# Graph layer on one core: the edge pass's hand-overs between TensorE, ScalarE and VectorE one third of a group later, a fourth one-hot buffer, chunks mixed from the middle third only

## Chip, cores and metric

The kernel runs on one NeuronCore of a Trainium2 chip. The metric is device time in microseconds. Before the change three runs took 1643.68, 1644.55 and 1645.81 us (median 1644.55). In the profile PE is TensorE (PEld its weight loads), ACT ScalarE, DVE VectorE, POOL GpSimd and SP SyncE; PEq, ACTq, DVEq, POOLq and SPq are their sequencers. "remote" and "another core or an unknown queue" both stand for a wait whose ending signal the profile can't put down to one instruction.

## The reference

There are 6250 nodes with 256 features and 106,250 edges sorted by destination. One layer computes

```
xn  = layernorm(x)
m   = xn[src] @ W[:256] + edge_attr @ W[256:]             # per edge
h   = segment_sum(m * rsqrt(degree)[dst], dst) + bias      # graph part
mix = gelu((q (K^T V)/N + xn) @ w1 + b1) @ w2 + b2 + xn    # linear attention, K and V normed per head
x   = x + h + mix
x   = x + expert_ffn(layernorm(x))                         # 2 of 8 experts, one choice for all nodes
```

The sum over edges is linear, so the kernel sums the raw gathered and edge rows by destination first and multiplies by W afterwards.

## The kernel before

There are three stages: a prologue (norms, a table of normed rows in memory), the edge pass, and the expert network. The change is in the edge pass.

**Steps and groups.** A strip is 128 x 3 edges, 4 strips make a group `t`, and there are 70 groups. A group has three steps, `q = 3t + i` with `i` 0, 1, 2. For a step SP loads four edge tiles (one DMA of 512 KB, line 423) and POOL gathers four tiles of 128 rows of 1 KB (four indirect DMAs, line 596) into one slot `q % 6` of a ring of six. PE multiplies the slot with one-hot matrices (`strip_sums`, lines 907 to 921) and then signals `s_seg`. SP and POOL may fill a slot again when `s_seg` says that the step six earlier is done (`wait_past(..., s_seg, q - RS + 1)`).

**What follows a group.** The group's sums stand in one of two PSUM banks. ACT copies them to `fl` (`evict`), PE transposes `fl` (`transposes`, line 927), ACT copies that to `fl_t` (`evict_t`), PE multiplies by W into the bank `ps_y` (`project`, lines 941 and 933, signals `s_pj`), and DVE adds the columns of `ps_y` to `acc` at a place read from a register (`sums`, line 1270, signals `s_acc`). The one-hot tiles `s32` are written by DVE for the next group (`one_hot`, line 1242), in three buffers.

**Work laid into the same steps.** Up to step 106 a tile of 125 nodes goes through keys and values every second step: `turn_kv` on PE, `turned` on ACT, `turned_lo` on DVE, `keys` on PE (line 986), `centred` on DVE, `squares` on ACT (line 704), `variances`, `deviations`, `normed`, `accumulate` on PE (992, 994). A short stretch folds the weights. Then 25 chunks of 250 nodes are mixed: `turn_mix` (1007), `turned`, `turned_lo`, `mix_first` (1020), `gelus` (723), `mixed_lo` (1308), `mix_second` (1030), `mixed` (1313), `store_base`. 25 times a chunk whose edge sums are complete is finished (`node_columns` 1043 and 1049, `degree_rows` 1359, `node_rows`, `row_scales`, `turn_rows` 1059 and so on).

**What sets the order.** Each engine runs its own copy of one loop over `q` and takes its instructions strictly in the order written there. `kv_at(q, lag)` and `mix_at(q, lag)` say which tile or chunk is `lag` steps old at `q`, `fin_at(t, lag)` the same in groups. So a number in the loops says in which step an engine turns to a piece of work, and what is written behind it in that step waits with it. Before the change in a group's steps:

```
        PE                                          ACT                       DVE
i = 0   sums, transposes(t-1)                       evict(t-1)                one_hot(t+1)
i = 1   sums, wait for acc, project(t-1)            evict_t(t-1)
i = 2   sums                                                                  sums(t-1)
```

A tile's transposes and keys are one step apart on PE (lags 0 and 1), a chunk's first and second product two (1 and 3). `MIX` holds the steps at which chunks begin: 114, 117, 121, 124, 128, 132, 135, 141, 144, ..., 201, from the eighth one on always at `i` = 0.

Of the kernel before, what the change touches and what calls it, by code (L numbers as in the profile page):

```python
# [14 lines left out]
P = 128  # L15
# [40 lines left out]
FOLD = KV0 + 2 * NT + 4  # L56
# [8 lines left out]
for c in range(NC):  # L65
    MIX.append(max(TS * FIRST - 3 + TS * 6 * c // 5, TS * (FIN[c - XC] + 5) if c >= XC else 0))
# [11 lines left out]
def gps_layer(nc, x, src_l, dst_l, edges, wgnn, hbias, wkv_l, wq_t, bkv_l, bq_l, kln_g, kln_b, vln_g, vln_b,  # L78
              w1, b1_l, w2, b2, wr, br, fw1, fb1_l, fw2, fb2, gamma, beta, out):
    ctx = ExitStack()  # L80
    with ctx:
# [34 lines left out]
        s32 = sbe("s32", [P, 3, GT, W], F32R)  # L116
# [539 lines left out]
        def _(act):  # L656
# [116 lines left out]
            for q in range(TS * STEPS):  # L773
# [17 lines left out]
                if kv_at(q, 3) is not None:  # L791
                    deviations(kv_at(q, 3))
# [6 lines left out]
                if mix_at(q, 5) is not None:  # L799
                    store_base(mix_at(q, 5))  # L800
# [95 lines left out]
        def _(pe):  # L896
# [12 lines left out]
            def strip_sums(q):  # L909
# [8 lines left out]
                for j in strips(t):  # L918
                    mm = pe.matmul(ps_seg[t % 2][j * W:(j + 1) * W, :], lhsT=s32[:, t % 3, j * TS + i, :].bitcast(F32), rhs=ring[:, u, j, :],  # L919
                                   start=i == 0, stop=i == TS - 1, skip_group_check=True)  # L920
# [16 lines left out]
            def project(t):  # L937
                n = W * len(strips(t))
                hot = s32[:, t % 3, :, :].rearrange("p (j i) w -> p j i w", i=TS)
# [122 lines left out]
            for q in range(TS * STEPS):  # L1062
# [3 lines left out]
                if i == 0 and 1 <= t <= NG:  # L1066
                    transposes(t - 1)
                if i == 1 and t:
                    columns_free(t)
                    if fin_at(t, 0) is not None:  # L1070
                        pe.wait_ge(s_acc, min(strips_before(DONE[fin_at(t, 0)]), NS))
                        node_columns(fin_at(t, 0))
                if i == 1 and 1 <= t <= NG:
                    if t == 1:
                        pe.wait_ge(s_par, 16 * 11)
                    project(t - 1)
                if kv_at(q, 5) is not None:
                    accumulate(kv_at(q, 5))
                if kv_at(q, 0) is not None:
                    turn_kv(kv_at(q, 0))  # L1080
                if kv_at(q, 1) is not None:
                    keys(kv_at(q, 1))
                if q in (FOLD + 1, FOLD + 3, FOLD + 5):
                    fold_weights((q - FOLD) // 2)
                if mix_at(q, 3) is not None:
                    mix_second(mix_at(q, 3))
                if mix_at(q, 0) is not None:
                    turn_mix(mix_at(q, 0))
                if mix_at(q, 1) is not None:
                    mix_first(mix_at(q, 1))  # L1090
                if i == 2 and fin_at(t, 2) is not None:
                    turn_rows(fin_at(t, 2), mixes_turned(q))

# [91 lines left out]
        def _(v):  # L1185
# [51 lines left out]
            def one_hot(t):  # L1237
# [3 lines left out]
                wait_past(v, s_pj, t - 2)  # L1241
                v.tensor_tensor(s32[:, t % 3, 0:m, :], iota[:, 0:W].unsqueeze(1).broadcast_to([P, m, W]),
# [156 lines left out]
            for q in range(TS * STEPS):  # L1399
# [5 lines left out]
                if i == 0 and fin_at(t, 1) is not None:  # L1405
                    node_rows(fin_at(t, 1))
                if kv_at(q, 4) is not None:
                    normed(kv_at(q, 4))
                if kv_at(q, 2) is not None:
                    centred(kv_at(q, 2))  # L1410
                if kv_at(q, 3) is not None:
                    variances(kv_at(q, 3))
                if i == 2 and 1 <= t <= NG:
                    v.wait_ge(s_pj, t)
# [219 lines left out]
```

## Time and profile before

| | |
|---|---|
| Profiled execution, own time | 1625.46 us |
| Its span, first to last instruction | 1623.7 us |
| Median of the timed runs | 1644.55 us |
| Mean granted TensorE clock | 0.868 of full speed |
| Busy over the span | PE 1182.9, POOL 935.0, DVE 637.4, ACT 546.5 us |
| Gathers (POOL, line 596) | 831, 803.3 us busy, 967 ns each, first at 52.0, last at 1275.2 us |
| One-hot products (PE, line 919) | 1662, 294.5 us busy |
| Projection (PE, line 933) | 1120, 157.2 us busy |
| Expert network (lines 1145 and 1156) | from about 1336 us to the end |

A row of the timeline gives start and length in us, engine, line, operation, what it writes and reads, how many were merged, and in brackets how long the engine sat idle before it and what ended that. A row of the waits gives who waited for whom, the total in us, the number and the longest.

### The profile page before, as it was taken

What the parts mean: (1) busy time and instruction counts of PE and PEld (TensorE: products, weight loads), DVE (VectorE), ACT (ScalarE), POOL (GpSimd) and SP (SyncE); (2) the same over time, 40 slices, a digit from 0 to 9 for tenths busy, and PEclk for the clock granted to TensorE, in tenths of its full rate; (3) what the DMA queues carried; (4) which work ended last, traced back from release to release, by engine and by line L of the source; (5) the groups of instructions that cost most, each with busy time, mean ns of one, the idle gap of its engine ahead of it and who ended that gap; (6) DMA issues with size and microseconds to landing.
All of it is one profiled execution on the core that took longest, in us unless ns stands there. A gap on an engine that the chain in (4) does not pass through costs nothing.

```text
span 1623.7 us, 22761 instructions
## 1 busy us (share of the span) xinstructions
PE 1182.9 (73%) x7416; PEld 804.4 (50%) x7416; DVE 637.4 (39%) x1619; ACT 546.5 (34%) x1126; POOL 935.0 (58%) x1005
## 2 busy tenths in 40 slices
PE   0257777677768676766676767777777839999997
PEld 0024344334334343334444544453554539999997
DVE  6113232233233233312234333342342446676775
ACT  5401111111111111111233333432443457677674
POOL 6566666666666666666666666666666103334342
PEclk9968888888889887877788788899887959999999
DMA  9956666666666666476677777777877341222221
GB/s 271 291 173 185 181 198 200 181 188 194 192 193 192 195 188 187 146 234 212 203 224 236 247 230 234 245 225 252 243 234 236 104 136 39 74 59 76 66 66 39
DMA packets 209236, 295.04 MB, mean 182 GB/s; under 512 B 20940, under 2 KB 180146, under 8 KB 207887
## 3 DMA queue, kind: packets, MB, share of 16 engines
q1 hardware_dynamic: 152899, 165.66, 34.4%
q0 software_dynamic: 39888, 108.97, 22.1%
q10 hardware_dynamic: 16350, 19.20, 3.6%
q8 instruction: 48, 0.79, 0.2%
q14 instruction: 51, 0.42, 0.1%
HBM read 261.75 MB, written 32.00 MB: 181 GB/s over the span
## 4 chain that ended last, share of the span: by engine, by line
PE 31%; another core or an unknown queue 27%; issue 19%; ACT 8%; DVE 8%; DMA 2%; DVEq 2%; SPq 1%; POOL 1%; ACTq 0%; POOLq 0%
PE bank L1145 8%; PE bank L1156 8%; PE bank L919 3%; PE bank L933 2%; PE bank L1030 2%; DVEq L1268 2%; ACT fl L658 2%; PE bank L927 1%; DVE lnst L1287 1%; PE bank L986 1%; ACT L743 1%; ACT L723 1%; ACT fl_t L658 1%; PE bank L992 1%
## 5 line engine op out<-in xcount | busy, mean ns | idle before, releaser
L596 POOL DMA_INDIRECT ring<-xn_table,src_sb x831 | 803.3, 967 | 431.8 <-issue 232.0
L919 PE MATMUL bank<-ring,s 128*32 128x512 f32 x1662 | 294.5, 686 | 72.2 <-DMA ring<-xn_table,src_sb 49.1
L933 PE MATMUL bank<-fl_t,wg 128*128 128x128 f32 x1120 | 157.2, 298 | 38.3 <-issue 24.9
L933 PEld LDWEIGHTS bank<-fl_t,wg 128*128 128x128 f32 x1120 | 144.9, 209 | 42.2 <-issue 26.6
L1270 DVE TENSOR_TENSOR acc<-acc,bank 128x96 f32 x277 | 70.7, 255 | 224.5 <-issue 86.2
L927 PE MATMUL bank<-ident,fl 128*128 128x128 f32 x280 | 58.1, 343 | 136.8 <-ACT fl L658 114.6
L927 PEld LDWEIGHTS bank<-ident,fl 128*128 128x128 f32 x280 | 37.3, 170 | 215.8 <-ACT fl L658 151.2
L1275 DVE TENSOR_TENSOR xt_lo<-bank,xt_hi 128x250 fp32r<-128x250 f32 (+1 forms) x75 | 37.8, 505 | 270.0 <-ACT xt_hi L658 195.4
L658 ACT ACTIVATE xt_hi<-bank 128x250 fp32r<-128x250 f32 (+1 forms) x75 | 33.4, 445 | 297.9 <-remote 237.3
L919 PEld LDWEIGHTS bank<-ring,s 128*32 128x32 f32 x1662 | 43.0, 114 | 169.0 <-issue 163.0
L1145 PE MATMUL bank<-xf_hi,fw_hi 128*128 128x256 f32 x400 | 113.6, 284 | 9.5 <-DVE fw_lo L1572 7.2
L986 PE MATMUL bank<-wkv_hi,xt_hi 128*125 128x512 f32 x100 | 56.4, 564 | 87.1 <-DVE xt_lo L1275 87.1
L704 ACT ACTIVATE kvn<-xc 125x512 f32<-125x512 f32 x50 | 31.5, 630 | 259.8 <-DVE xc L1283 131.0
L647 POOL TENSOR_TENSOR rx<-vex,half 125x2 f32<-125x2 f32 x25 | 17.7, 707 | 171.9 <-DVE nmx L1546 171.9
L1525 DVE TENSOR_TENSOR h_lo<-h,h_hi 128x512 fp32r<-128x512 f32 x100 | 95.7, 968 | 48.7 <-ACT h_hi L658 48.7
L1145 PE MATMUL bank<-xf_lo,fw_hi 128*128 128x256 f32 x400 | 113.8, 284 | 0.0
L1145 PE MATMUL bank<-xf_hi,fw_lo 128*128 128x256 f32 x400 | 113.4, 283 | 0.0
L1156 PE MATMUL bank<-fw_hi,h_hi 128*125 128x256 f32 x400 | 111.7, 279 | 0.0
L1156 PE MATMUL bank<-fw_hi,h_lo 128*125 128x256 f32 x400 | 111.7, 279 | 0.0
L1156 PE MATMUL bank<-fw_lo,h_hi 128*125 128x256 f32 x400 | 111.6, 279 | 0.0
L844 ACT ACTIVATE h<-bank,fb1c 128x256 f32<-128x256 f32 x200 | 83.4, 468 | 73.2 <-PE bank L1145 72.7
L1283 DVE TENSOR_TENSOR xc<-bank,bkv 125x512 f32<-125x512 f32 x50 | 34.6, 692 | 147.4 <-remote 70.1
(213 smaller groups left out, 2349.7 us busy)
## 6 DMA issues: line engine op xcount, KB each, us to landing
ring<-edges SPq DMA_DIRECT2D x207, 512.0 KB
ring<-xn_table,src_sb POOLq DMA_INDIRECT x831
xnr<-xn_table SPq DMA_DIRECT2D x50, 125.0 KB
xnr<-xn_table SPq DMA_DIRECT2D x25, 250.0 KB
xch<-x SPq DMA_DIRECT2D x25, 250.0 KB
base_rows<-xch ACTq DMA_DIRECT2D x25, 250.0 KB
x_rows<-xch ACTq DMA_DIRECT2D x25, 250.0 KB
xt_cols<-xte ACTq DMA_DIRECT2D x25, 250.0 KB
```

Of the source, the lines that this page charges most:

```text
L596: pool.indirect_dma_start(out=to, out_offset=None, in_=table, in_offset=bass.IndirectOffsetOnAxis(ap=index, axis=0),).then_inc(done, 16)
L658: return nc.scalar.activation(o, i, ACT.Copy)
L844: nc.scalar.activation(h32[:, f, :], bank[q][:, (f % 2) * CW:(f % 2 + 1) * CW], ACT.Gelu, bias=fb1c[:, f:f + 1]).then_inc(s_gel, 1)
L919: mm = pe.matmul(ps_seg[t % 2][j * W:(j + 1) * W, :], lhsT=s32[:, t % 3, j * TS + i, :].bitcast(F32), rhs=ring[:, u, j, :], start=i == 0, ...
L927: mm = pe.transpose(ps_t[:, c * P:(c + 1) * P], fl[:, c * P:(c + 1) * P], ident[:, :])
L933: mm = pe.matmul(ps_y[:, o * P:(o + 1) * P], lhsT=wg[:, c, o * P:(o + 1) * P], rhs=fl_t[:, c, :], start=c == 0, stop=c == 3)
L986: mm = pe.matmul(ps_kv[0:TN, :], lhsT=a, rhs=b, start=i == 0, stop=i == len(ops) - 1)
L1145: mm = pe.matmul(bank[q][:, (f % 2) * CW:(f % 2 + 1) * CW], lhsT=a, rhs=b, start=n == 0, stop=n == len(ops) - 1)
L1156: mm = pe.matmul(ps_o[u][0:TN, j * D:(j + 1) * D], lhsT=a, rhs=b, start=n == 0, stop=n == len(ops) - 1)
L1270: v.tensor_tensor(acc[:, :, ds(b, W)], acc[:, :, ds(b, W)], ps_y[:, 0:3 * P].rearrange("p (c n) -> p c n", c=3)[:, :, j * W:(j + 1) * W], ...
L1275: v.tensor_tensor(xt_lo[:, :, 0:width], ps_xt[:, 0:KC * width].rearrange("p (c n) -> p c n", c=KC), xt_hi[:, :, 0:width].bitcast(F32), ALU ...
L1525: v.tensor_tensor(h_lo[:, u, 2 * q:2 * q + 2, :], h32[:, 2 * q:2 * q + 2, :], h_hi[:, u, 2 * q:2 * q + 2, :].bitcast(F32), ALU.subtract).t ...
```

## The change

Each hand-over inside the group and inside a tile or chunk is asked for later, the one-hot tiles get a fourth buffer (`HOT = 4`, the wait in `one_hot` becomes `s_pj >= t - 3`), and `MIX` becomes 115, 118, 121, 124, 127, 133, 136, 142, ..., 202: always at `i` = 1. `FOLD` is one step later. PE's wait for `acc` before the projection is split off: `columns_free` waits only for `s_acc`, the degree signal `s_dr` is waited for before `project` alone.

```
        PE                                          ACT                       DVE
i = 0   sums, ..., project(t-2) last in the step    evict(t-1)                one_hot(t+1)
i = 1   sums, transposes(t-1)                                                 ..., sums(t-2) last
i = 2   sums, node_columns                          evict_t(t-1)
```

A tile's lags on PE are now 0, 2 and 6 (before 0, 1 and 5), a chunk's 0, 2 and 5 (before 0, 1 and 3); ACT and DVE move with them. What each operation computes, the DMAs, their sizes and the ring of six are as before.

```diff
-FOLD = KV0 + 2 * NT + 4
+HOT = 4
+FOLD = KV0 + 2 * NT + 5
-    MIX.append(max(TS * FIRST - 3 + TS * 6 * c // 5, TS * (FIN[c - XC] + 5) if c >= XC else 0))
+    MIX.append(max(TS * (FIRST + c + c // 5) - 2, TS * (FIN[c - XC] + 5) + 1 if c >= XC else 0))
@@ ACT
-                if i == 1 and 1 <= t <= NG:
+                if i == 2 and 1 <= t <= NG:
                     evict_t(t - 1)
-                if i == 1 and fin_at(t, 1) is not None:
+                if i == 2 and fin_at(t, 1) is not None:
                     store_rows(fin_at(t, 1))
-                if kv_at(q, 2) is not None:
-                    squares(kv_at(q, 2))
+                if kv_at(q, 3) is not None:
+                    squares(kv_at(q, 3))
-                if mix_at(q, 2) is not None:
-                    gelus(mix_at(q, 2))
+                if mix_at(q, 3) is not None:
+                    gelus(mix_at(q, 3))
@@ PE
-                wait_past(pe, s_acc, strips_before(min(t, NG - 1) - 1) if t < NG else strips_before(NG - 1) + (1 if t > NG else 0))
-                wait_past(pe, s_dr, sum(g < t for g in FIN))
+                wait_past(pe, s_acc, min(strips_before(t), NS))
-                if i == 0 and 1 <= t <= NG:
+                if i == 1 and 1 <= t <= NG:
                     transposes(t - 1)
-                if i == 1 and t:
-                    columns_free(t)
-                    if fin_at(t, 0) is not None:
-                        pe.wait_ge(s_acc, min(strips_before(DONE[fin_at(t, 0)]), NS))
-                        node_columns(fin_at(t, 0))
-                if i == 1 and 1 <= t <= NG:
-                    project(t - 1)
-                if kv_at(q, 5) is not None:
-                    accumulate(kv_at(q, 5))
+                if i == 2 and fin_at(t, 0) is not None:
+                    columns_free(t - 1)
+                    pe.wait_ge(s_acc, min(strips_before(DONE[fin_at(t, 0)]), NS))
+                    node_columns(fin_at(t, 0))
+                if kv_at(q, 6) is not None:
+                    accumulate(kv_at(q, 6))
+                if kv_at(q, 2) is not None:
+                    keys(kv_at(q, 2))
                 if kv_at(q, 0) is not None:
                     turn_kv(kv_at(q, 0))
-                if kv_at(q, 1) is not None:
-                    keys(kv_at(q, 1))
-                if mix_at(q, 3) is not None:
-                    mix_second(mix_at(q, 3))
+                if mix_at(q, 5) is not None:
+                    mix_second(mix_at(q, 5))
+                if mix_at(q, 2) is not None:
+                    mix_first(mix_at(q, 2))
                 if mix_at(q, 0) is not None:
                     turn_mix(mix_at(q, 0))
-                if mix_at(q, 1) is not None:
-                    mix_first(mix_at(q, 1))
+                if i == 0 and 2 <= t <= NG + 1:
+                    columns_free(t - 2)
+                    wait_past(pe, s_dr, sum(g < t for g in FIN))
+                    project(t - 2)
@@ DVE
-                wait_past(v, s_pj, t - 2)
+                wait_past(v, s_pj, t - HOT + 1)
-                if i == 2 and 1 <= t <= NG:
-                    v.wait_ge(s_pj, t)
-                if i == 2 and fin_at(t, 0) is not None:
-                    degree_rows(fin_at(t, 0))
-                if i == 2 and 1 <= t <= NG:
-                    sums(t - 1)
+                if i == 1 and 2 <= t <= NG + 1:
+                    sums(t - 2)
```

On DVE `degree_rows` moves to `i` = 0 of the following group, `node_rows` to `i` = 1, `normed`, `centred` and `variances` one step later each, `mixed` and `mixed_lo` two.

## Rows read from the trace of the kernel before

**Rows 1.** Windows: stretch, us; busy PE, PEld, DVE, ACT, POOL; clock, DMA, GB/s.

```profile
325.00:500.00 175.00, 129.95 (x681) 68.57 (x682) 57.63 (x142) 27.93 (x66) 114.55 (x120) 0.84 0.64 192
...
745.00:920.00 175.00, 123.10 (x750) 79.40 (x750) 57.55 (x170) 53.02 (x102) 115.99 (x119) 0.80 0.73 223
...
920.00:1095.00 175.00, 129.60 (x798) 83.71 (x795) 64.90 (x194) 65.40 (x135) 114.92 (x118) 0.89 0.77 236
```

**Rows 2.** Waits of POOL, whole execution: us in total, times, longest.

```profile
POOL ring L596 <- issue: 232.0, 738, 1.0
...
POOL ring L596 <- remote: 142.7, 67, 5.2
...
POOL ring L596 <- PE bank L919: 46.1, 25, 4.7
```

**Rows 3.** Waits of all engines, 150 to 1265 us.

```profile
ACT xt_hi L658 <- remote: 223.7, 35, 13.5
...
ACT hm L723 <- remote: 136.0, 16, 14.2
...
PE bank L927 <- ACT fl L658: 112.8, 34, 9.3
...
PE bank L986 <- DVE xt_lo L1275: 86.5, 15, 7.7
```

**Rows 4.** Timeline, 422 to 431 us, keys-and-values stretch.

```profile
422.08 0.38 PE L975 MATMUL bank<-ident,xnr 125*128 125x125 f32 x2
...
422.39 1.06 PE L919 MATMUL bank<-ring,s 128*32 128x512 f32 x8
...
426.74 0.95 POOL L596 DMA_INDIRECT ring<-xn_table,src_sb  x1 [0.30 <-issue]
...
430.04 0.38 ACT L658 ACTIVATE xt_hi<-bank 128x250 fp32r<-128x250 f32 x1 [9.72 <-remote]
...
430.37 0.94 POOL L596 DMA_INDIRECT ring<-xn_table,src_sb  x1 [2.68 <-remote]
...
430.93 0.79 PE L986 MATMUL bank<-wkv_hi,xt_hi 128*125 128x512 f32 x1 [6.00 <-DVE xt_lo L1275]
```

**Rows 5.** The timeline, 447 to 450 us, the next group.

```profile
447.60 0.69 DVE L1283 TENSOR_TENSOR xc<-bank,bkv 125x512 f32<-125x512 f32 x1 [7.08 <-remote]
...
449.12 0.59 ACT L658 ACTIVATE fl<-bank 128x512 f32<-128x512 f32 x1
...
449.76 1.12 PE L927 MATMUL bank<-ident,fl 128*128 128x128 f32 x4 [3.90 <-ACT fl L658]
```

**Rows 6.** The timeline, 1012 to 1034 us, mixing stretch.

```profile
1012.13 0.60 ACT L658 ACTIVATE fl<-bank 128x512 f32<-128x512 f32 x1 [9.78 <-remote]
...
1012.88 0.66 PE L927 MATMUL bank<-ident,fl 128*128 128x128 f32 x4
...
1029.70 0.83 ACT L723 ACTIVATE hm<-bank,bm 128x250 f32<-128x250 f32 x2 [9.66 <-remote]
...
1032.61 0.58 ACT L658 ACTIVATE fl<-bank 128x512 f32<-128x512 f32 x1
...
1033.24 1.11 PE L927 MATMUL bank<-ident,fl 128*128 128x128 f32 x4 [1.77 <-ACT fl L658]
```

**Rows 7.** The timeline, 419 to 421 us: one projection on PE.

```profile
419.85 0.55 PE L941 MATMUL bank<-s,ones_r 128*128 128x128 f32 x3
...
420.24 2.00 PE L933 MATMUL bank<-fl_t,wg 128*128 128x128 f32 x16
```

**Rows 8.** The chain that ended last: start us, us, what.

```profile
813.35 2.12 PE bank L1020 x12
...
1050.24 2.56 PE bank L1030 x12
...
1335.97 7.42 PE bank L1145 x48
```

**Rows 9.** The timeline, the last gather.

```profile
1275.18 0.94 POOL L596 DMA_INDIRECT ring<-xn_table,src_sb  x1 [4.72 <-PE bank L919]
```

More of the change, by code:

```diff
@@ L115, in gps_layer @@
         ring = sbe("ring", [P, RS, ST, 2 * D])
-        s32 = sbe("s32", [P, 3, GT, W], F32R)
+        s32 = sbe("s32", [P, HOT, GT, W], F32R)
         ones_r = sbe("ones_r", [P, P], F32R)
@@ L786, in _ @@
                     norm_rows(fin_at(t, 2))
-                if kv_at(q, 2) is not None:
-                    squares(kv_at(q, 2))
+                if kv_at(q, 3) is not None:
+                    squares(kv_at(q, 3))
                 if kv_at(q, 0) is not None:
                     turned(kv_at(q, 0), TN)
-                if kv_at(q, 3) is not None:
-                    deviations(kv_at(q, 3))
+                if kv_at(q, 4) is not None:
+                    deviations(kv_at(q, 4))
                 if q == FOLD + 6:
                     mix_weights()
-                if mix_at(q, 2) is not None:
-                    gelus(mix_at(q, 2))
+                if mix_at(q, 3) is not None:
+                    gelus(mix_at(q, 3))
                 if mix_at(q, 0) is not None:
                     turned(NT + mix_at(q, 0), CN)
-                if mix_at(q, 5) is not None:
-                    store_base(mix_at(q, 5))
+                if mix_at(q, 7) is not None:
+                    store_base(mix_at(q, 7))
                 if i == 2 and fin_at(t, 1) is not None:
@@ L918, in strip_sums @@
                 for j in strips(t):
-                    mm = pe.matmul(ps_seg[t % 2][j * W:(j + 1) * W, :], lhsT=s32[:, t % 3, j * TS + i, :].bitcast(F32), rhs=ring[:, u, j, :],
+                    mm = pe.matmul(ps_seg[t % 2][j * W:(j + 1) * W, :], lhsT=s32[:, t % HOT, j * TS + i, :].bitcast(F32), rhs=ring[:, u, j, :],
                                    start=i == 0, stop=i == TS - 1, skip_group_check=True)
@@ L938, in project @@
                 n = W * len(strips(t))
-                hot = s32[:, t % 3, :, :].rearrange("p (j i) w -> p j i w", i=TS)
+                hot = s32[:, t % HOT, :, :].rearrange("p (j i) w -> p j i w", i=TS)
                 for i in range(TS):
@@ L1405, in _ @@
                 if i == 0 and fin_at(t, 1) is not None:
+                    degree_rows(fin_at(t, 1))
+                if i == 1 and fin_at(t, 1) is not None:
                     node_rows(fin_at(t, 1))
+                if kv_at(q, 5) is not None:
+                    normed(kv_at(q, 5))
+                if kv_at(q, 3) is not None:
+                    centred(kv_at(q, 3))
                 if kv_at(q, 4) is not None:
[L1408 to L1412, printed above, removed]
-                if i == 2 and 1 <= t <= NG:
-                    v.wait_ge(s_pj, t)
-                if i == 2 and fin_at(t, 0) is not None:
-                    degree_rows(fin_at(t, 0))
-                if i == 2 and 1 <= t <= NG:
-                    sums(t - 1)
+                    variances(kv_at(q, 4))
                 if kv_at(q, 0) is not None:
@@ L1422, in _ @@
                     fold((q - FOLD) // 2)
-                if mix_at(q, 4) is not None:
-                    mixed(mix_at(q, 4))
+                if mix_at(q, 6) is not None:
+                    mixed(mix_at(q, 6))
                 if mix_at(q, 1) is not None:
                     base_rows(mix_at(q, 1))
-                if mix_at(q, 2) is not None:
-                    mixed_lo(mix_at(q, 2))
+                if mix_at(q, 4) is not None:
+                    mixed_lo(mix_at(q, 4))
                 if mix_at(q, 0) is not None:
                     turned_lo(NT + mix_at(q, 0), CN)
+                if i == 1 and 2 <= t <= NG + 1:
+                    sums(t - 2)
             v.wait_ge(s_acc, NS)
```

6 lines of the change are left out of this document (3 added, 3 removed).

## The prediction

> **What bounds the kernel now.** I read the page first for the stages, then the windows, the waits of POOL, the waits of all engines, and last the timeline of single groups. The expert network begins at 1336 us with PE in one unbroken row [rows 8] and is not touched, so all that can move is the edge pass, from the first gather at 52.0 to the last at 1275.2 us [rows 9]. That is 831 gathers, 69.25 groups of 12, and so 17.66 us a group. The windows show no engine full: of 175 us (ten groups) PE is busy 123 to 130, POOL 115, ACT 28 to 65, DVE 58 to 65, the DMA engines 0.64 to 0.77 [rows 1]. PE's busy time is the same 12 to 13 us a group in both halves, and so is the group's time.
>
> POOL is nearest to a floor. A gather takes 967 ns on average (the page) and 0.30 us lie between two [rows 4], so 12 of them need 15.2 us. The rest is in its waits for a ring slot: 142.7 us ended by "remote" and 46.1 by the one-hot products, 92 waits in all [rows 2]. Both are the same wait, for `s_seg`. Less the 0.30 us that stands between gathers anyway, 188.8 - 92 x 0.30 = 161 us. That is the most the change can win as long as POOL issues 831 gathers.
>
> So POOL waits for PE. Does PE wait for data? No: it is six steps behind POOL, a full ring. The timeline shows what it does wait for. At 422.08 it turns a tile (0.38 us), at 422.39 it sums a step, but ACT takes the turned tile up only at 430.04, POOL its slot at 430.37, and PE's keys start at 430.93 [rows 4]. Such late answers are the largest waits of the pass: ACT on the turned tile 223.7 us in 35 waits, ACT on the chunk's first product 136.0 in 16, PE on `fl` 112.8 in 34, PE on `xt_lo` 86.5 in 15 [rows 3]. I take two parts in them apart: the time until PE's signals are out (here 430.0, when ACT and POOL go on within 0.4 us of each other), and the time after it in which PE stands until ACT and DVE have answered.
>
> **The change part by part.** No work is added to the loops but the width of one buffer. Every instruction, DMA and wait on a ring slot is there as often as before; the price of the moves is in waits alone.
>
> *Hand-overs.* PE asks now for `fl` after the next step's sums instead of in front of them, for `fl_t` two steps and not one after `fl`, and for `xt_lo` two steps after the turn. What goes is the stand after the signals are out. Its size, from single groups: 430.93 - 430.04 = 0.9 us (keys) [rows 4]; 449.76 - 447.60 = 2.2 us, the chain DVE `xc`, ACT square, ACT `fl` [rows 5]; in the mixing stretch 1012.88 - 1012.13 = 0.75 and 1033.24 - 1029.70 = 3.5 us, the latter with ACT's gelus, a table load and a root in front of `fl` [rows 6]. The mean is 1.5 us a group over the 31 groups from 150 to 700 us and 2.1 over the 30 from 745 to 1265: 47 + 63 = 110 us. The low end of this term is 0: if POOL's wait ends only with the burst of signals, PE's earlier idling costs nothing. The high end is the whole of POOL's waits, 161 us. I take half of the 110, 55 us, because the two groups in rows 4 and 5 both show POOL released in the burst itself (430.37, and DVE at 447.60), and not by a step of its own that PE did after waiting for ACT; only what PE has done before the next burst counts, and that is where a shorter stand helps.
>
> *Projection last in step 0, sums last in step 1, fourth one-hot buffer.* The projection takes 0.55 + 2.00 us with the small gap between, 2.4 us [rows 7], as before. DVE's four additions begin one step later than the projection instead of in the next but one place; `one_hot(t+1)` waits for projection t-2, which then stands 3 steps back, so it waits for nothing. Cost 0 beside the ring; without the fourth buffer DVE would wait at each group's start for the projection that PE does at the end of that very step. The bounds are a gain of 0.5 us a group, if DVE's order was late, and a loss of the same: 0 +- 30 us. I take 0.
>
> *Chunks.* `mix_second`, `mix_first` and the projection now all stand in step 0: sums 1.06, second 2.56, first 2.12, projection 2.4 [rows 4, 7, 8] make 8.1 us in which one slot comes free, against 5.0 us for POOL's four gathers of a step. Before, the longest such stretch was step 1 with sums, projection and first product, 5.6 us. The sum per group is the same, and the other two steps become shorter; it costs nothing as long as the ring has a slot in hand, and up to 2.5 us a chunk if it has none, 25 x 2.5 = 63 us. I take 0 for the likeliest case because the stretch after it is shorter by as much, and keep the 63 for a rival.
>
> *SP.* `mix_load` is asked for at step `MIX[c]`, its three waits (turns, `base_rows` of two chunks ago, stored rows of six chunks ago) keep their distance in steps; edge loads queue behind it as before. 0.
>
> *End.* Two steps later for the last group's projection and additions, on a nearly idle machine: between the last gather at 1275.2 and the network at 1336 lie 61 us. One projection and four additions stand in the way at most once more, some 5 us. On the other side PE is less far behind when the gathers end. I take +5.
>
> Sum: -55 + 0 + 0 + 5 = -50 us. The profiled execution took 1625.5 us by its own time, 19 us less than the median of the timed runs, 1644.55, and no difference in the stages is seen for it here; I subtract the 50 from the median: **1595 us** (profiled: 1575).
>
> Two rules of the Trainium skill bear on the split. The page "SBUF — State Buffer", section "SBUF: two separate sides", says that DMA and the engines reach SBUF by separate ports and cannot slow each other. By that rule the 7.6 us in rows 4 between PE's turn and ACT's copy are no matter of the gathers in flight, all waits are hand-over, and the second rival below is the likeliest; the trace does not plainly agree, since at 422.4 to 430.0 ACT and PE had nothing else to do. "Perfetto Trace Analysis", section "Optimization Strategy", says that the same gap repeating on an engine that should be full can mean too few buffers for the next tile. POOL's repeating wait agrees with it, the ring keeps its six slots, and by this rule nothing is won: the first rival.
>
> **The rivals.**
>
> *The waits come back elsewhere (the ring decides).* POOL waits 92 times in 69 groups, 2 us at a time on average, in the stretch of keys as in that of chunks, although the work on PE, ACT and DVE is quite different [rows 1, 2]. That speaks for a cycle of its own: ring full, POOL stops, PE's signals come in a burst, POOL goes on. Then a group stays at 17.6 us and the time at 1640 to 1650. Against it: in both bursts shown PE stood idle before it, so more could have been done by then.
>
> *POOL becomes the bound.* Every hand-over has a whole step of 5 us now, more than the answers measured. If that ends most of POOL's waits, a group takes 15.2 to 16 us, -161 to -100 with the end: 1488 to 1545, say 1525. For it: PE's 12 to 13 us of work fit into 15.2. Against it: the 7.6 us for PE's signals in rows 4 are longer than one step, and moving work doesn't shorten them.
>
> *Slower: step 0 too full.* The mechanism is the 8.1 us of PE work in step 0 of the mixing stretch. It decides when PE's slot signals are still a full ring behind at that point, which the waits say they are in nearly all groups before. Then POOL waits up to 2.5 us more in each chunk, up to 63 us, against at best a part of the 63 us that shorter hand-overs give there; and the 47 us of the first half come only in part if the signals are late. Taken at a third of the 63 with nothing won elsewhere, +21: 1665; at most 1705. The smaller idle time of PE against it would have to be seen in the first half.
>
> **How the numbers follow.** Chances: forecast 0.43 (its own range 1560 to 1620); POOL the bound 0.14; ring decides 0.20; step 0 too full 0.18; the moves do little things of either sign, within 20 us, 0.05. A measurement of this kernel tells 0.2% (3.3 us) from no change. Of the ring case 0.12 lie within that, 0.05 on the faster side and 0.03 on the slower; the last case is shared. Faster 0.43 + 0.14 + 0.05 + 0.03 = 0.65, same 0.12, slower 0.18 + 0.03 + 0.02 = 0.23. The range leaves out the lower half of POOL the bound and the worse half of step 0 too full: 1522 to 1664.
>
> **What would show it.** Right: POOL's waits on line 596 other than "issue" fall from 189 us to some 130; last gather near 1225 us; PE no longer waits for `fl` and `xt_lo` (199 us now) but the copies on ACT still start late after PE; a group 16.9 us. The ring case: the waits for `fl` and `xt_lo` go, POOL's stay at 189, PE's idle time moves to other lines or in front of line 919. POOL the bound: last gather before 1180 us. Step 0 too full: the windows before 700 us no longer than now, those after 745 us longer, POOL's waits there ended by line 919 and longer than the 4.7 us of now. I am wrong altogether if DVE or ACT show a new long wait, on `s_acc`, on `s_dr` or on a root, in front of the projection.

## The result and the profile after

The changed kernel takes 1667.69 us (median, 1663.83 to 1670.97) against 1644.12 for the kernel before beside it: a ratio of 1.0159, 95% interval 1.0138 to 1.018, slower by 24 us by the medians and 26 by the ratio. The forecast was 1595. All comparisons leave out one execution, of e18's kernel, that took 2598.55 us where its others took 1494 to 1504. The profiled execution after took 1667.02 us, near its median; the one before, 1625.46, was 19 us quicker than its own, so the two traces show 41.5 us of difference where some 25 are to be explained.

By stage, read from the starts of POOL's gathers (from a group's first gather to another group's first gather, and the last gather) and of DVE's mean over the nodes, which the expert network waits for. The labels e1 to e18 are the experiments told below; "quick set" is explained at e14.

| us | group 0 to 35 | 38 to 68 | last gather to mean | mean to end |
|---|---|---|---|---|
| before | 611.2 | 532.5 | 33.0 | 315.5 |
| before, a second profile (e7) | 609.4 | 530.8 | 33.2 | 315.0 |
| after | 618.2 | 547.2 | 51.2 | 314.8 |
| e1, group's part | 614.4 | 547.4 | 46.4 | 314.4 |
| e2, keys' part | 614.7 | 537.6 | 33.0 | 315.2 |
| e3, chunks' part | 617.5 | 535.2 | 43.2 | 315.1 |
| e4, additions first | 613.8 | 540.8 | 51.9 | 315.2 |
| e5, projection first too | 608.3 | 535.2 | 50.9 | 316.4 |
| e6, chunks earlier | 610.8 | 540.7 | 41.3 | 316.3 |
| e9, all three moves | 613.9 | 542.1 | 43.1 | 314.9 |
| e10, keys' part, chunks earlier | 614.1 | 547.6 | 33.0 | 315.6 |
| e12, before, ring of five | 615.4 | 541.7 | 32.5 | 315.3 |
| e14, before, half rows, quick set | 535.0 | 459.1 | 27.3 | 314.3 |
| e16, keys' part, quick set | 534.4 | 476.4 | 35.4 | 315.4 |
| e18, changed, quick set | 536.5 | 478.5 | 50.8 | 314.8 |

The tail after the last gather is the steadiest item: +18 us. The two long stretches are not steady. The kernel before, e12 and e10 time alike (within 0.1% of each other), and yet their first stretch differs by up to 6 us and their second by up to 17 (530.8 to 547.6). The 547.2 us of the changed kernel lie inside that, so one profile's stretch does not show a loss of this size. What does is the timed ratio less the tail: 26 - 18 leaves some 8 us, with the ratio's interval 4 to 11, for everything in front of the last gather.

The windows of the kernel after, the same stretches as in [rows 1] (stretch; busy time of PE, weight loads, DVE, ACT, POOL; clock, DMA share, GB/s):

```profile
325.00:500.00 175.00, 134.31 (x673) 67.45 (x666) 57.12 (x140) 26.78 (x65) 113.84 (x119) 0.85 0.62 188
745.00:920.00 175.00, 113.57 (x675) 72.12 (x674) 52.97 (x155) 49.80 (x94) 112.36 (x118) 0.79 0.72 215
920.00:1095.00 175.00, 127.61 (x769) 83.96 (x769) 60.18 (x182) 62.37 (x127) 108.88 (x113) 0.79 0.78 230
```

From 920 to 1095 us POOL does less than before (108.88 us busy, 114.92 before) and TensorE's granted clock is lower, 0.79 against 0.89.

POOL's gathers as a group (count; busy, mean ns of one; idle before them and its causes):

```profile
L597 POOL DMA_INDIRECT ring<-xn_table,src_sb x831 | 801.0, 964 | 458.4 <-issue 224.8 <-remote 125.8 <-PE bank L920 94.1
```

The waits other than "issue" were 142.7 + 46.1 = 188.8 us [rows 2] and are 219.9. The waits from 150 to 1265 us, beside [rows 3]:

```profile
ACT xt_hi L659 <- remote: 229.5, 25, 17.3
...
PE bank L1043 <- issue: 65.7, 12, 7.9
...
DVE xch L1378 <- DMA base_rows<-xch: 51.8, 8, 10.8
...
PE bank L1043 <- DVE acc L1271: 46.2, 9, 8.6
...
ACT hm L724 <- remote: 27.6, 5, 10.2
```

PE's waits for `fl` and for the keys' `xt_lo` (199 us) are gone, as intended. In their place PE stands in front of line 1043, `node_columns`, 112 us here. That line over the whole execution, before and then after:

```profile
L1043 PE MATMUL bank<-ones,acc 1*125 1x1 f32 x100 | 14.9, 249 | 2.4 <-DVE acc L1270 2.4
...
L1043 PE MATMUL bank<-ones,acc 1*125 1x1 f32 x100 | 22.8, 328 | 122.9 <-issue 67.9 <-DVE acc L1271 55.0
```

The idle time in front of it was 2.4 us and is 122.9. The timeline shows why. DVE, 1128 to 1140 us of the kernel after:

```profile
1130.53 0.88 DVE L1378 SCALAR_TENSOR_TENSOR xch<-bank,norm,xch 125x256 f32<-125x256 f32 x2 [9.11 <-DMA base_rows<-xch]
...
1135.21 0.26 DVE L1271 TENSOR_TENSOR acc<-acc,bank 128x96 f32 x1 [1.88 <-issue]
1136.34 0.25 DVE L1271 TENSOR_TENSOR acc<-acc,bank 128x96 f32 x1 [0.87 <-issue]
1137.36 0.26 DVE L1271 TENSOR_TENSOR acc<-acc,bank 128x96 f32 x1 [0.77 <-issue]
1138.24 0.26 DVE L1271 TENSOR_TENSOR acc<-acc,bank 128x96 f32 x1 [0.62 <-issue]
```

and PE in the same stretch:

```profile
1127.76 1.06 PE L934 MATMUL bank<-fl_t,wg 128*128 128x128 f32 x8
...
1138.55 0.99 PE L1043 MATMUL bank<-ones,acc 1*125 1x1 f32 x4 [7.16 <-DVE acc L1271]
```

The projection ends at 1128.8. Its four additions end at 1138.5, because DVE takes them last in the step: `node_rows` stands in front (it waits 9.11 us for the store of the chunk's base rows, which ACT now issues two steps later in the chunk's order), then `mixed`. PE's `node_columns` waits for all four. Before the change it stood three steps behind the projection whose additions it waits for, and two behind DVE's place for them; now it stands two and one behind. In 23 of the 25 chunks the chunk's own sums have been complete for longer (`DONE` lies two groups or more before `FIN` in the kernel): the wait is for the bank alone, since the two degree columns lie in `ps_y`, which DVE is reading. The Trainium skill, "PSUM — Partial Sum Buffer", section "PSUM bank collisions raise a hardware error", says that two engines may not be on one bank and partition quadrant at once and that the hardware doesn't arbitrate; no run here puts these columns into another bank.

The tail before, from the last groups' additions to the mean:

```profile
1293.30 0.26 DVE L1270 TENSOR_TENSOR acc<-acc,bank 128x96 f32 x1 [0.49 <-DVE acc L1270]
1293.61 0.51 PE L941 MATMUL bank<-s,ones_r 128*128 128x32 f32 x3 [1.02 <-DVE acc L1270]
...
1297.86 0.56 PE L1043 MATMUL bank<-ones,acc 1*125 1x1 f32 x4 [1.86 <-DVE acc L1270]
...
1308.17 0.20 DVE L1468 TENSOR_REDUCE mean_c<-mean_p 128x2 f32<-128x50 f32 x1 [5.67 <-issue]
```

and after:

```profile
1329.59 2.00 PE L934 MATMUL bank<-fl_t,wg 128*128 128x128 f32 x16
...
1332.37 0.26 DVE L1271 TENSOR_TENSOR acc<-acc,bank 128x96 f32 x1 [0.84 <-PE bank L934]
...
1335.65 0.26 DVE L1271 TENSOR_TENSOR acc<-acc,bank 128x96 f32 x1 [0.65 <-DVE acc L1271]
...
1335.96 0.59 PE L942 MATMUL bank<-s,ones_r 128*128 128x32 f32 x3 [3.94 <-DVE acc L1271]
...
1341.16 0.56 PE L1043 MATMUL bank<-ones,acc 1*125 1x1 f32 x4 [1.18 <-DVE acc L1271]
...
1350.43 0.20 DVE L1467 TENSOR_REDUCE mean_c<-mean_p 128x2 f32<-128x50 f32 x1 [4.95 <-issue]
```

With no gathers left to hide behind, projection, additions, next projection, additions and `node_columns` run one after the other. From the last `node_columns` to the mean it is 10.3 us before and 9.3 after; the last gather comes 22.7 us ahead of that instruction before and 41.9 after.

### The profile page after: what moved, and what is told of

Its sections match the earlier page's. It is cut to its first block, busy times and chain, and to the rows that moved or that the text cites. A ratio compares the mean times of both kernels' runs of the same rounds, so it can differ in the third digit from the quotient of the medians.

```text
span 1665.2 us, 22736 instructions
## 1 busy us (share of the span) xinstructions
PE 1207.6 (73%) x7416; PEld 814.3 (49%) x7416; DVE 638.0 (38%) x1619; ACT 548.5 (33%) x1126; POOL 932.4 (56%) x1005
## 4 chain that ended last, share of the span: by engine, by line
PE 47%; issue 19%; another core or an unknown queue 15%; DVE 7%; DVEq 5%; ACT 4%; DMA 2%; POOL 1%; SPq 0%; ACTq 0%; POOLq 0%
PE bank L1146 8%; PE bank L1157 8%; PE bank L920 8%; DVEq L1269 4%; PE bank L934 4%; PE bank L987 4%; PE bank L1031 3%; PE bank L993 2%; DVE acc L1271 2%; PE bank L995 2%; PE bank L928 1%; PE bank L1049 1%; PE bank L1021 1%; PE bank L1043 1%
## 5 line engine op out<-in xcount | busy, mean ns | idle before, releaser
L920 PE MATMUL bank<-ring,s 128*32 128x512 f32 x1662 | 329.8, 728 | 114.5 <-issue 53.4
L920 PEld LDWEIGHTS bank<-ring,s 128*32 128x32 f32 x1662 | 51.9, 118 | 222.7 <-issue 213.8
L934 PE MATMUL bank<-fl_t,wg 128*128 128x128 f32 x1120 | 148.3, 288 | 0.0
L934 PEld LDWEIGHTS bank<-fl_t,wg 128*128 128x128 f32 x1120 | 139.1, 202 | 0.0
L648 POOL TENSOR_TENSOR rx<-vex,half 125x2 f32<-125x2 f32 x25 | 17.7, 707 | 171.8 <-DVE nmx L1545 171.8
L1043 PE MATMUL bank<-ones,acc 1*125 1x1 f32 x100 | 22.8, 328 | 122.9 <-issue 67.9
L993 PE MATMUL bank<-kvn,ones 125*1 125x512 f32 x100 | 66.4, 750 | 61.1 <-issue 31.9
L1043 PEld LDWEIGHTS bank<-ones,acc 1*125 1x125 f32 x100 | 20.8, 289 | 146.1 <-issue 81.3
L1146 PEld LDWEIGHTS bank<-xf_hi,fw_hi 128*128 128x128 f32 x400 | 76.6, 191 | 10.2 <-DVE fw_lo L1571 7.4
```

Of the source, the lines that this page charges most:

```text
L934: mm = pe.matmul(ps_y[:, o * P:(o + 1) * P], lhsT=wg[:, c, o * P:(o + 1) * P], rhs=fl_t[:, c, :], start=c == 0, stop=c == 3)
L993: pe.matmul(ps_f[0:1, :], lhsT=ones[0:TN, 0:1], rhs=kvn[:, n % 2, :], start=n == 0, stop=n == NT - 1, skip_group_check=True)
L1043: mm = pe.matmul(ps_y[0:TN, DEG + j:DEG + j + 1], lhsT=acc[0:1, KC, a:a + TN], rhs=ones[0:1, 0:1], start=True, stop=True)
L1146: mm = pe.matmul(bank[q][:, (f % 2) * CW:(f % 2 + 1) * CW], lhsT=a, rhs=b, start=n == 0, stop=n == len(ops) - 1)
```

## The experiments

The first four runs take the change apart; a kernel with none of the three parts is the kernel before but for the fourth buffer.

**e1, the group's part alone** (keys, chunks and `MIX` as before).

```
 ACT   evict_t, store_rows at i = 2          PE  transposes i = 1, node_columns i = 2, project(t-2) last in i = 0
 DVE   degree_rows i = 0, node_rows i = 1, sums(t-2) last in i = 1;  HOT = 4
```

> Only the group's part of the change: transposes, projection, node_columns, additions and evict_t at their new places, the fourth one-hot buffer; keys, chunks and MIX as in the kernel before. Late additions (node_columns at i = 2 waits for additions that DVE does last in i = 1, behind node_rows): the loss is here, +10 to +25 us against before, the wait of node_columns for acc is 50 us or more, and the pass loses mainly after 700 us. Step 0 too full: chunks are spread over all steps as before, so no loss, within 5 us. Ring cycle (POOL's wait once a group has its own length whatever the hand-overs): the stretch before 700 us unchanged within 5 us.

Measured: 1657.14 us against 1642.28, ratio 1.0084 (1.0056 to 1.0112), +14 us. The first stretch is unchanged within what profiles scatter, the tail is 46.4 us, and `node_columns` waits 78 us:

```profile
L1043 PE MATMUL bank<-ones,acc 1*125 1x1 f32 x100 | 18.7, 287 | 78.1 <-DVE acc L1271 40.4 <-issue 37.7
```

The late additions are in this part, as their 78 us of waits show, but of its 14 us some 13 are the tail's (46.4 against 33.0). So these waits alone cost the pass about nothing, give or take 5 us.

**e2, the keys' part alone** (`keys` at lag 2, `accumulate` 6, and what lies between one later).

> Only the key and value tiles' part: keys two steps after the turn, and what follows one step later (the fourth one-hot buffer is there too, but nothing waits for it). My prediction's hand-over term: the waits for xt_lo and fl in the first half shrink, -10 to -25 us. Ring cycle: within 4 us of before. Late additions and step 0 too full: they need the other parts, so nothing lost here.

Measured: 1638.15, ratio 0.998 (0.9962 to 0.9998), -3 us. The forecast's hand-over term, -10 to -25 here, missed.

**e16, the same in five rounds.**

> The key tiles' part alone once more, in five rounds: the only version so far with an interval below 1 (0.9962 to 0.9998). If that was real, 0.997 to 0.999 again; if it was chance, the interval holds 1.

Measured: ratio 0.9993 (0.997 to 1.0015). The keys' part can't be told from no change, and with it goes the only candidate for beating both kernels. This set was one of the quick ones, in which POOL hardly stops; for the others e10 below, which holds the same part, says the same.

**e3, the chunks' part alone** (`MIX` at i = 1, `mix_first` 2, `gelus` 3, `mixed_lo` 4, `mix_second` 5, `mixed` 6, `store_base` 7).

> Only the chunks' part: MIX always at i = 1, first product at lag 2, second at lag 5, the rest later; groups and keys as before (fourth one-hot buffer in place). Step 0 too full: the two products (4.7 us) still meet in step 0, the projection stands in step 1, so a part of the loss shows, +5 to +15 us, after 745 us. Late additions: node_columns does not wait behind node_rows here; what can be late is node_rows' own wait for the base rows' store, now two steps later: +0 to +8 us. Hand-over term: -10 to -30 us after 745 us.

Measured: 1646.69, ratio 1.0029 (1.0011 to 1.0046), +5 us, and it isn't in the pass but in the tail: 43.2 us against 33.0. The tail's 10 us are more than the whole loss, so the two products in one step cost the pass nothing. The three parts alone add up to +15 us by their ratios (13.8 + 4.8 - 3.3), the whole change is 26 in its own set: some 10 us come only from the parts together, give or take 7 by the intervals.

**e4, additions first.** The changed kernel with `sums(t - 2)` moved from the end of DVE's step to the place ahead of `turned_lo`.

> The changed kernel with one move: DVE does the group's additions in i = 1 before turned_lo, not after it and the chunk's base rows. Late additions behind turned_lo: node_columns' wait for acc falls from 120 us to under 60 and the time by 8 to 20 us. If node_rows' wait for the base rows' store is the larger part, since it still stands in front: only 0 to 5 us. Step 0 too full or ring cycle: no change within 4 us.

Measured: 1656.1, ratio 1.009 (1.0062 to 1.0119) against the changed kernel's 1.0159 in its own set, so 11 us of the 26 are back.

```profile
L1043 PE MATMUL bank<-ones,acc 1*125 1x1 f32 x100 | 19.2, 292 | 80.3 <-DVE acc L1271 52.8 <-issue 27.5
```

The time moved as late additions had it; the wait fell to 80 and not under 60. `node_rows` still stands in front of the additions.

**e5, projection first too.**

In PE's loop these lines move from the end of the step to the place right behind `strip_sums(q)`, and the additions stand as in e4 (cut at "..."):

```
                if i == 0 and 2 <= t <= NG + 1:
                    ...
                    project(t - 2)
```

> The changed kernel with two moves: the projection of the group stands right behind the sums of step 0, in front of the chunk's two products (4.7 us of PE work), and DVE does the additions in i = 1 before turned_lo. Late additions: node_columns gets back what it lacked, its wait for acc falls from 120 us to under 25 and the time by 12 to 22 us against the changed kernel, to about 1648 us; the tail stays long. Step 0 too full: the same work stands in step 0, so no gain over the run with the additions first (1656 us). Ring cycle: under 4 us off 1656.

Measured: 1639.15 against 1627.46, ratio 1.0066 (1.004 to 1.0092).

```profile
L1043 PE MATMUL bank<-ones,acc 1*125 1x1 f32 x100 | 17.9, 275 | 28.8 <-DVE acc L1271 26.3 <-issue 2.3
```

15 of the 26 us are back. This and e4 are told apart by the wait, not by the time: their ratios' intervals overlap. Step 0 of PE holds the same work in the changed kernel, in e4 and here, so its fullness can't be what these 11 to 15 us were. What is left, 11 us, is less than the tail's 17.7: in front of the last gather this kernel gains some 7 us on the kernel before (by the interval 3 to 11), and which of its moves gives them no run shows.

**e6, chunks up to a group earlier**: `TS * (FIN[c - XC] + 3) + 1`.

> The changed kernel with chunks mixed up to a group earlier (a chunk waits for the place FIN + 3 of six chunks before and not FIN + 5; the last one starts at 199 and not 202). Tail theory (after the last gather PE still has the last chunk's second product, its addition and its store in front of the last node rows): the stretch from the last gather to the mean falls from 51 us by 6 to 12. Late additions: the pass up to the last gather does not change by more than 5 us. If the tail is only the group's own chain, no change there.

Measured: the tail falls from 51.2 to 41.3 us as expected, the time doesn't: ratio 1.0158 (1.0141 to 1.0175), as for the changed kernel in its own set. If the two sets can be compared, what the tail gave was lost in front of the last gather; where, this run doesn't show.

**e9, all three moves together.**

> The changed kernel with the additions first on DVE, the projection first in step 0 (as in the run before the last ones, +0.66% against before) and chunks mixed up to a group earlier (which took 10 us off the tail). If the two causes are separate, their gains add: 0.0 to +0.3% against before. If the earlier chunks only move work into the pass, as the timed median of their own run hints, +0.5 to +0.8%.

Measured: 1651.27 against 1638.13, ratio 1.0082 (1.0056 to 1.0108); tail 43.1 us, `node_columns` 16 us of waits. Set beside e6, the two moves give 12 us (1.0158 to 1.0082), so their gain is there a second time; it is the earlier chunks that give nothing. This run also bears on a rival that no run tests, the granted clock: it was 0.852 to 0.861 in the changed kernel's runs, 0.864 to 0.883 in those of the kernel before in the set of e1 to e4, and 0.875 to 0.885 here, where 13 us are still lost. In e3 the mixing stretch has a clock of 0.81 (0.86 before, 0.79 after; 745 to 1265 us) and the pass is not longer. No run holds the clock still, so what part of the changed kernel's 26 us it makes isn't shown.

**e10**, the keys' part with the earlier chunks:

> The kernel before with the key tiles' new lags (alone: -0.2%) and chunks mixed earlier (FIN + 3), at their old lags and order. A candidate for beating both kernels: the tail of before, 33 us, still holds the last chunk's store and node rows; if the last chunk's mixing is a part of it, the tail falls by 2 to 6 us and the whole is at -0.3 to -0.6%; if the tail is the group's own chain, -0.2%.

Measured: ratio 1.0008 (0.9986 to 1.0029), tail 33.0. No version tried beats the kernel before.

**What holds a group.** e7 is the kernel before again, for a second profile (1619.53 us; its stages are in the table). The expectation of longer stretches was wrong: this profile is as quick as the first.

> The kernel before, unchanged, for a second profile: the first one was 19 us faster than the median of its timed runs. If that run was simply a quick one, the second profile shows the key stretch (groups 0 to 35) and the mixing stretch (38 to 68) some us longer, 611 to 618 and 533 to 545, and the same tail of 33 us.

**e12, a ring of five**, and **e11, eleven gathers of twelve** in the kernel before:

```diff
@@ e12
-RS = 6
+RS = 5
@@ e11 (PE's count of arrived gathers is lowered to match)
-                for j in strips(t):
+                for j in [j for j in strips(t) if not (q >= RS and i == 2 and j == 3)]:
```

> The kernel before with a ring of five slots. Ring decides (POOL stops because its slot is not yet given back, PE's signals late behind gathers in flight): 0.5 to 1.5 us more a group, 35 to 105 us. POOL's own rate decides: under 10 us more.

> The kernel before with one gather of each group's twelve left out (the fourth tile of step 2; its half of the sum is then of old rows). POOL and its gathers set the group's length: 17.6 us falls by one gather's share, 1.2 to 1.5 us a group, 85 to 105 us in all. The burst cycle with a fixed stall: the same 1.27 us of POOL's work may be taken up by a longer stall, so the group falls by under 0.5 us.

Measured, one execution each: e12 1636.97 and e11 1551.92 against 1638.13. POOL's gathers in e12:

```profile
L596 POOL DMA_INDIRECT ring<-xn_table,src_sb x831 | 810.7, 976 | 436.9 <-issue 228.9 <-remote 140.4 <-PE bank L919 56.9
```

and in e11:

```profile
L596 POOL DMA_INDIRECT ring<-xn_table,src_sb x764 | 746.3, 977 | 415.1 <-issue 201.8 <-remote 115.1 <-PE bank L919 87.5
```

With a slot less the stops are 197 us (189 before) and the time is the same: the ring doesn't decide. With 67 gathers less the time falls by 86 us, 1.29 each, a gather's 0.967 + 0.30; the stops stay (203 us). The gathers set the group, with a stop of some 2 us about once a group on top that neither the slot nor the gather left out changed. The Trainium skill's rule that I had set beside [rows 2], that a repeating gap can mean too few buffers ("Perfetto Trace Analysis", section "Optimization Strategy"), doesn't hold for this gap by the run with five; a ring of more than six was not run.

**e8 and e17, the kernel before without gathers** after the first six steps (half of each sum is then of old rows), **e13, the changed kernel likewise.**

The count that PE waits for is lowered to match.

```diff
-                for j in strips(t):
+                for j in strips(t) if q < RS else ():
```

> The kernel before with the gathers left out after the first six steps (the gathered half of the sums is then of old rows), everything else as it was. POOL is out of the loop, the edge loads remain. If PE's signals come late because of gathers in flight (ring cycle), a group falls from 17.6 us to PE's own 12 to 14. If the hand-overs between PE, ACT and DVE were what holds a group, as my forecast had it, it stays at 16 or more.

> The changed kernel with the gathers left out after the first six steps, to set beside the same cut of the kernel before (1211.7 us; no stops of POOL at all). The loss is in the order itself (late additions, longer tail): node_columns waits for acc as with gathers, 3 to 6 us in most of its 25, and the whole is 15 to 30 us longer than 1211.7. The loss needs POOL and its gathers: within 8 us of 1211.7 but for the tail.

> The kernel before without gathers once more (after the first six steps), because the changed kernel without gathers (1351.9 us) ran on another chip than this one's first run (1211.7 us). If the difference of 140 us is the order of the two kernels, this is within 1% of 1212 whatever the chip. If it was the chip, it lies nearer 1350.

Measured: 1211.66, 1351.89 and 1209.37 us, one execution each. The first was taken in a set in which the kernel before needs 1627 us, the third in one in which it needs 1481: without gathers the two kinds of sets agree. The windows of e17:

```profile
150.00:500.00 350.00, 329.20 (x2103) 177.50 (x2106) 168.06 (x424) 83.74 (x193) 0.00 (x0) 1.00 0.53 155
600.00:850.00 250.00, 212.46 (x1587) 150.33 (x1586) 127.86 (x389) 130.73 (x269) 0.00 (x0) 0.92 0.69 211
```

and of e13:

```profile
150.00:500.00 350.00, 309.57 (x1956) 174.74 (x1952) 162.04 (x401) 76.57 (x185) 0.00 (x0) 0.98 0.47 139
600.00:950.00 350.00, 264.67 (x1792) 180.66 (x1791) 139.11 (x437) 145.25 (x298) 0.00 (x0) 0.83 0.57 168
```

By the starts of PE's sums a group takes 11.4 us (keys) and 12.0 (mixing) in e17, 12.2 and 15.5 in e13. The order written in the kernel before can run a third faster than it does with the gathers; the changed order can't in the mixing stretch, and its `node_columns` alone waits

```profile
L1043 PE MATMUL bank<-ones,acc 1*125 1x1 f32 x100 | 20.8, 308 | 92.3 <-DVE acc L1271 92.3
```

against 1.9 in e17. So the loss lies in the order itself and needs no gathers. It is 140 us, where 15 to 30 were expected; with the gathers 26 are left. Not all of the 140 is waiting: the mixing stretch of e13 also has the lower clock, 0.83 against 0.92, and PE is busy 11.7 us a group there against 10.2 (from the windows), 1.5 of the 3.5 us.

**e14, gathered rows of 512 bytes** (half of each gathered row, from another place) and **e15, fills by POOL in place of the gathers** (the gathered half is constant).

> The kernel before with gathered rows of 512 bytes and not 1 KB (half of each gathered row is fetched, from another place of the table; the other half of the slot is old). Same number of gathers, same PE work. The stops of POOL come from the transfers (landing late): they shrink, by 60 us or more in all. They belong to the number of gathers or to the order of PE, ACT and DVE: within 20 us of 1638, gathers at about 0.97 us each as before.

> The kernel before with each gather after the first six steps replaced by eight small fills of the same part of the slot by POOL (no transfer; the gathered half is then constant). POOL's own work in the loop, PE's wait for it and the ring stay, only the indirect transfers go. PE's late signals and POOL's stops come with the indirect transfers: PE's turned tile is answered by ACT within 2 us in nearly all cases, POOL's stops sum to under 40 us while POOL is the slower side, and a group takes 12 times POOL's own time for four fills' worth. They are a matter of POOL being busy or of the ring: the stops and the late answers stay as in the kernel before.

Measured: e14 1451.66, e15 1236.29; the kernel before beside them took 1484.21, not 1640. In this set and in the next (1481.25), the quick sets, POOL has hardly a stop in any profile. One of these is e16, whose time can't be told from the kernel before's; of the kernel before itself there is no profile in such a set. So e14 and e15 can't say what the stops are. In e15 a group is bound by PE (POOL waits 403 us for it). e14 does say what sets a group where POOL doesn't stop: with half the bytes the first stretch is as long as in e16 (535.0 and 534.4 us, 15.3 a group; 12 gathers at 0.968 + 0.30 are 15.2), so there it is the number of gathers. In the mixing stretch and the tail the smaller rows give 17 and 8 us beside e16.

The sets also answer whether PE's late signals [rows 4] belong to this kernel's order. In the trace before, of the 38 tiles that ACT takes up between 150 and 600 us, 18 are taken up more than 3 us after PE has turned them. In e16 and e18 it is none of 43 each, with all the gathers in flight, and in e8, without gathers but in a slower set, none of 48. One such pair of e16, beside 422.08 and 430.04 in rows 4:

```profile
427.10 0.38 PE L976 MATMUL bank<-ident,xnr 125*128 125x125 f32 x2
...
427.52 0.38 ACT L659 ACTIVATE xt_hi<-bank 128x250 fp32r<-128x250 f32 x1 [10.99 <-PE bank L976]
```

So the lateness comes with the gathers and only in the slower sets; the order makes neither.

**e18, the changed kernel in such a set.**

> The changed kernel once more, with a profile, beside the kernel before on this chip. On a chip on which POOL stops once a group (before at 1625 to 1645 us): 1.012 to 1.018 as before, tail 51 us. On a chip without those stops (before at 1484 us, groups of 15.2 us, POOL never short of a slot): PE and DVE have 2.4 us a group less cover, so node_columns' wait of some 5 us a chunk shows more: 1.02 to 1.05, lost in the mixing stretch and the tail.

Measured: 1496.2 (median of four) against 1481.25, ratio 1.0083 (1.0057 to 1.0109). Its windows and one of its waits, with POOL at its pace until group 56:

```profile
150.00:500.00 350.00, 274.12 (x1568) 154.37 (x1568) 134.23 (x326) 63.17 (x152) 266.21 (x276) 0.90 0.74 220
650.00:900.00 250.00, 183.28 (x1197) 121.64 (x1196) 89.74 (x271) 90.39 (x178) 189.66 (x199) 0.82 0.83 251
```

```profile
DVE xch L1378 <- DMA base_rows<-xch: 117.5, 15, 13.1
```

I expected 1.02 to 1.05, since the shorter group leaves less cover, and that was wrong: `node_columns` waits 52 us, but the mixing stretch is 478.5 us against 476.4 in e16, and the loss is the tail, 50.8 against 35.4 us. These waits cost the pass next to nothing. That a full ring swallows them here, and that POOL's stops have already spent it in the slower sets, fits but isn't shown.

## Why the prediction was wrong

- **The hand-over term, -55 us, failed.** I saw PE stand 1.5 to 2.1 us a group after its signals [rows 4 to 6], each a mean of two single groups, and took half of that as time by which slots come free. The waits for `fl` and `xt_lo` went from 199 us to none and POOL's waits rose from 189 to 220. Keys' part alone: -3 us, then -1 with an interval that holds 0. Without gathers the old order needs 11.4 to 12.0 us for a group that takes 17.6, so those 110 us lay inside time in which PE had nothing due. Its low end, 0, was right, and its reason stood in the text: if the wait ends only with the burst of signals, PE's earlier idling costs nothing.
- **"Projection last in step 0, sums last in step 1": 0 +- 30, was the second failure, of mechanism more than of size.** I followed the new order only to `one_hot`, which waits for the projection, and to the next projection, which waits for the additions. `node_columns` waits for the additions too. Its slack fell by a step, and `node_rows` with its wait for a store moved into the same DVE step in front of them. Measured: 123 us of waits on line 1043, and 11 to 15 us back by two moves that only bring the additions forward (12 in e9 beside e6). The waits are no measure of the loss: e1 has 78 us of them and loses next to nothing outside the tail. That a new long wait for `s_acc` would overturn the forecast stood there, but "in front of the projection"; it is in front of line 1043.
- **End, +5: mis-sized.** It is +18 in the profiles (+15 in e18). I counted one projection and four additions; the later group costs 13 us and the later chunks 10, where together they give 18. The tail's 18 and the 11 to 15 us of the moves are more than the 26 together. If the sets can be compared, the rest of the change gains a few us somewhere; where isn't shown.
- **Chunks in step 0, 0: right for the pass** (e3, whose whole loss is the tail's). The rival built on it, step 0 too full, gave 1665 us, next to the measured 1667.69, by luck: e4 and e5 keep step 0 as full and have 11 and 15 us back.
- **The ring rival** was right that the stretch of keys stays and that POOL's waits don't follow the hand-overs; the ring isn't what decides, as e12 shows.
- **The 161 us of removable stops are real in size**: in the sets without them the kernel before takes 1484 and 1481 us, 143 to 163 less. No change of order here removed them.
- **PE's late signals.** The forecast took the 7.6 us of rows 4 as given and looked only at what follows them. By e8, e16 and e18 they are there with gathers and in the slower sets alone. The reading that they are no matter of the gathers in flight fails there; what makes them is open.

Open as well: where e6 and e9 lose in the pass what their tails gain, and the 10 us that the parts cost only together. For these there is a hint: DVE waits 51.8 us for the base rows' store in the changed kernel, 14.0 in e3, and no wait is put down to it in e1, where the chunks keep their places. But e4 and e5 still have that wait and are quicker.

## What to carry to other kernels

When a result is handed over later, list every instruction that waits for it, not only the one for which it was moved: here `node_columns` lost a step of slack, while the waits that went had cost nothing. Run the order once without the engine that bounds the loop; 11.4 against 17.6 us a group would have shown that no hand-over there was worth touching, and 15.5 against 12.0 that the new order is worse. A pipeline made deeper by a third of a group also costs at its end, where nothing covers it: 18 us here, and 15 even where the loop itself lost only some 5 (e18 beside e16). And a long new wait in a trace is not yet a loss: 78 us of it cost the pass nothing in e1.

## What the runs showed of the hardware

- The same kernel took 1627 to 1644 us in four sets of runs and 1481 to 1484 in two others. A group took 17.6 us in its profile and, up to the mixing stretch, 15.3 in e16's; a gather is as long in both (967 and 968 ns). The difference is in POOL's stops. Chip number 8 ran one set of either kind, so the number doesn't separate them. What does isn't shown. The keys' part in the quick kind (e16):

```profile
L597 POOL DMA_INDIRECT ring<-xn_table,src_sb x831 | 804.7, 968 | 287.3 <-issue 246.7 <-PE bank L920 26.7 <-DMA xn_table<-acc 13.9
```

- Where POOL makes its stops, about 2 us once a group, their sum didn't follow the ring (five slots: 197 us in all, six: 189) nor one gather in twelve left out (203 us).
- In the slower sets ACT takes up a turned tile late in 18 of 38 cases (over 3 us) when gathers are in flight; never in the quick sets, nor without gathers.
- The changed kernel's ratio was 1.0159 in a slower set and 1.0083 in a quick one, where little but the tail is left of the loss.
